# Merging normalizations into their consumers, moving one more copy of the heads to ScalarE, and batching small vector instructions

## What is computed

```python
x = x + 0.5 * moe(layernorm(x))         # 64 experts, top 8 of a sigmoid router, plus a shared expert
x = x + heads(layernorm(x))             # 16 heads of 8 features; softmax(y y^T / sqrt(8)) @ x, then a 2048 x 128 weight
x = x + 0.5 * moe(layernorm(x))
x = x + 0.5 * cells(layernorm(x))       # gated cell over 4 steps, then tanh output
x = x + decayed_attention(layernorm(x)) # with its own second normalization and a 128-512-128 mlp
x = x + 0.5 * cells(layernorm(x))
```

## Time and profile before

| what | value |
|---|---|
| median of three runs | 2742.0 us (2739.37 to 2742.69) |
| the profiled execution, time | 2743.51 us |
| its span | 2741.4 us |
| mean granted TensorE clock | 0.966 |
| PE, DVE, ACT, POOL busy | 93%, 81%, 66%, 45% of the span |
| moe normalization and routing, twice | from 5.85 to 88.3 us and from 1663.8 to 1740.2 us |
| experts, twice | to about 617 and 2269 us |
| heads, tiles | 657 to 1660 us |
| cells, twice; decayed attention; mlp | the rest |

### The profile page before, as it was taken

One profiled execution on the slowest core, in us unless ns is written; L12 is line 12 of the kernel. 1 busy time (PEld: TensorE's weight loads), 2 busy tenths in 40 slices (PEclk: granted clock), 3 DMA queues, 4 the chain that ended last, 5 costly groups with the idle time before them and its releaser, 6 DMA issues. The chain is left out here.

```text
span 2741.4 us, 35099 instructions
## 1 busy us (share of the span) xinstructions
PE 2545.0 (93%) x11075; PEld 1905.2 (69%) x11075; DVE 2223.1 (81%) x3277; ACT 1821.2 (66%) x3026; POOL 1231.3 (45%) x1265
## 2 busy tenths in 40 slices
PE   6899999996999999999999997899999998788778
PEld 3688888874666666666666664688888885476556
DVE  6778777776999999999999996777787775567655
ACT  3455555556888888888888884455555555557665
POOL 3466666664323232332323322466666662245401
PEclk9999999998999999999999999999999999888999
DMA  3566666644333333333333321566666640100000
GB/s 85 118 138 145 145 142 135 136 103 164 98 107 99 106 102 97 109 100 104 104 103 101 98 93 34 127 144 138 135 146 145 143 105 8 32 16 8 8 8 31
DMA packets 107385, 271.47 MB, mean 99 GB/s; under 512 B 30784, under 2 KB 35648, under 8 KB 107072
## 3 DMA queue, kind: packets, MB, share of 16 engines
q1 hardware_dynamic: 82192, 235.42, 34.7%
q0 software_dynamic: 24576, 33.62, 4.4%
q10 hardware_dynamic: 432, 0.20, 0.0%
HBM read 258.35 MB, written 10.76 MB: 98 GB/s over the span
## 5 line engine op out<-in xcount | busy, mean ns | idle before, releaser
L614 POOL TENSOR_TENSOR moe_experts_lo<-moe_experts_hidden,moe_experts_hi 128x512 fp32r<-128x512 f32 x512 | 661.1, 1291 | 340.6 <-ACT moe_experts_hi L552 340.4
L895 DVE TENSOR_TENSOR heads_e_lo<-heads_e,heads_e_hi 128x1024 fp32r<-128x1024 f32 x512 | 616.1, 1224 | 25.7
L559 ACT ACTIVATE psum<-psum 128x512 f32<-128x512 f32 x512 | 298.0, 582 | 479.8 <-PE psum L90 479.8
L729 POOL DMA_DIRECT2D heads_left<-heads_parts x512 | 306.5, 612 | 671.3 <-PE psum L783 610.7
L835 ACT ACTIVATE heads_e<-psum 128x1024 f32<-128x1024 f32 x512 | 520.0, 1023 | 108.2 <-PE psum L783 108.2
L586 DVE TENSOR_TENSOR moe_experts_weighted<-moe_spread,psum 128x512 f32<-128x512 f32 x512 | 350.8, 685 | 190.2 <-PE psum L90 186.4
L88 PE MATMUL psum<-heads_e_hi,heads_v_lo 128*128 128x512 f32 x1024 | 429.4, 419 | 18.0 <-DVE heads_u L861 18.0
L88 PE MATMUL psum<-moe_n_hi,moe_w_lo 128*128 128x512 f32 x1024 | 400.8, 391 | 4.2 <-PEq L54 3.9
L89 PE MATMUL psum<-heads_e_lo,heads_v_hi 128*128 128x512 f32 x1024 | 404.2, 395 | 0.0
L90 PE MATMUL psum<-heads_e_hi,heads_v_hi 128*128 128x512 f32 x1024 | 400.9, 391 | 0.0
L89 PE MATMUL psum<-moe_n_lo,moe_w_hi 128*128 128x512 f32 x1024 | 400.2, 391 | 0.0
(11 more groups left out here) (403 smaller groups left out, 4093.8 us busy)
## 6 DMA issues: line engine op xcount, KB each, us to landing
moe_spread<-moe_mask SPq DMA_DIRECT2D x128, 1024.0 KB, 9.8
heads_right<-heads_parts SPq DMA_DIRECT2D x512, 64.0 KB
heads_left<-heads_parts POOLq DMA_DIRECT2D x512, 64.0 KB, 2.5
heads_scale<-heads_inverse_copy SPq DMA_DIRECT2D x64, 512.0 KB, 3.7
moe_experts_raw<-in_gate SPq DMA_DIRECT2D x16, 256.0 KB, 11.7
moe_experts_raw<-in_up SPq DMA_DIRECT2D x16, 256.0 KB, 11.8
moe_experts_raw<-in_down SPq DMA_DIRECT2D x16, 256.0 KB, 11.6
heads_parts<-heads_e_hi SPq DMA_DIRECT2D x16, 256.0 KB, 3.2
```

The lines of the kernel that those rows point to most:

```text
L559: act.activation(psum[:, GATE + p % 2, :], psum[:, GATE + p % 2, :], ACT.Silu).then_inc(silu_ready, 1)
L614: pool.tensor_tensor(lo[:, p, :], hidden[:, p % 2, :], f(hi[:, p, :]), ALU.subtract).then_inc(low_ready, 1)
L729: eng.dma_start(f(tile[row:row + 2 * HEAD, h % 2, :]), parts_dram[dims, order:order + 2, at]).then_inc(loaded[h % 2], 16)
L895: dve.tensor_tensor(e_lo[:, s, :], e[:, s % 4, :], f(e_hi[:, s, :]), ALU.subtract).then_inc(low, 1)
```

## The change

- The normalization becomes a class `Norm` whose parts are called inside the stage that uses it, for routing, cells and mlp (five places). The heads and decayed attention keep the separate stage. Of its 8 PSUM banks it uses 6 (two for variances), and the stages' banks are arranged so that their first products find free ones. Chunk 0's low part moves from GpSimd to VectorE everywhere; in the moe layers the splits of the first experts' weights move behind the low parts.
- In routing, the first products run before the normalization's last chunks are done, the mask copy moves to ScalarE, and selection uses one instruction for four tiles where it used four (chosen, scaling); the sum of the best eight is a reduction of its own.
- In the heads, tile 4's high part moves from VectorE to ScalarE, and the three steps on u use one instruction of 1024 columns in place of two of 512.

```diff
 # normalization
-    BANKS = 4
-    VECTOR_LOWS = (2, 5, 7)
+    CENTERS, VARIANCES = 4, 2
+    VECTOR_LOWS = (0, 2, 5, 7)
+        for i in range(self.early):
+            split(i)
+        for c in range(CHUNKS):
+            if c not in self.VECTOR_LOWS:
+                self.take_low(pool, "pool", c)
+        for i in range(self.early, len(self.splits)):
+            split(i)
+    def wait_banks(self, eng):
+        eng.wait_ge(self.scaled_ready, CHUNKS)
+        eng.wait_ge(self.logs_taken, CHUNKS)
 # routing, TensorE
+                norm.tensor(pe)
+                norm.wait_weights(pe)
+                pe.wait_ge(norm.scaled_ready, LOGITS + 5)
                 logits(0, 0)
+                pe.wait_ge(norm.log_ready, CHUNKS)
+                shared(0, 0)
+                norm.wait_banks(pe)
                 turn_affinity(0, 0)
                 each_chunk(step)
 # routing, ScalarE
+                def copy_mask(c, j):
+                    act.wait_ge(routed_turned, c + 1)
+                    after(act, mask_stored[j], 16 * (c // 2))
+                    act.copy(mask[:, j, :], psum[0:EXPERTS, MASK, :]).then_inc(mask_ready, 1)
                 def step(c, j, last):
                     if not last:
                         affinities(c + 1, 1 - j)
+                    if c > 0:
+                        copy_mask(c - 1, 1 - j)
                     act.wait_ge(up_ready, c + 1)
 # routing, VectorE
-                    for q in range(4):
-                        dve.scalar_tensor_tensor(out=chosen[:, j, q, :], in0=rest[:, j, q, :], scalar=0.0,
-                                                 in1=scores(q), op0=ALU.is_lt, op1=ALU.mult,
-                                                 accum_out=total[:, j, q:q + 1]).then_inc(chosen_ready, 1)
+                    dve.tensor_reduce(total[:, j, :], best[:, j, :, :], mybir.AxisListType.X, ALU.add).then_inc(total_found, 1)
+                    dve.scalar_tensor_tensor(out=chosen[:, j, :, :], in0=rest[:, j, :, :], scalar=0.0,
+                                             in1=psum[:, TURNED + j, :].rearrange("p (q t) -> p q t", q=4)[:, :, 0:EXPERTS],
+                                             op0=ALU.is_lt, op1=ALU.mult).then_inc(chosen_ready, 1)
-                    for q in range(4):
-                        dve.tensor_scalar(routed[:, j, q, :], chosen[:, j, q, :], total[:, j, q:q + 1], None,
-                                          ALU.mult).then_inc(routed_ready, 1)
+                    dve.tensor_tensor(routed[:, j, :, :], chosen[:, j, :, :],
+                                      total[:, j, :].unsqueeze(2).to_broadcast([P, 4, EXPERTS]), ALU.mult).then_inc(routed_ready, 1)
-                    dve.tensor_copy(mask[:, j, :], psum[0:EXPERTS, MASK, :]).then_inc(mask_ready, 1)
 # heads
-        ACT_HIGH = (1, 3, 5, 7)
+        ACT_HIGH = (1, 3, 4, 5, 7)
-                    pe.wait_ge(u_low, (g + 1) * HALVES)
+                    pe.wait_ge(u_low, g + 1)
-                            after(pe, scaled_ready, (h - 1) * HALVES + half + 1)
+                            after(pe, scaled_ready, h)
-                    for half in range(HALVES):
-                        act.wait_ge(scaled_ready, g * HALVES + half + 1)
-                        act.copy(u_hi[:, g % 2, half, :], u[:, half, :]).then_inc(u_high, 1)
+                    act.wait_ge(scaled_ready, g + 1)
+                    act.copy(u_hi[:, g % 2, :], u[:, :]).then_inc(u_high, 1)
-                    for half in range(HALVES):
-                        after(dve, u_low, (g - 1) * HALVES + half + 1)
-                        dve.tensor_tensor(u[:, half, :], scale[:, g % 2, half * BANK:(half + 1) * BANK],
-                                          psum[:, OUT + half, :], ALU.mult).then_inc(scaled_ready, 1)
+                    after(dve, u_low, g)
+                    dve.tensor_tensor(u[:, :], scale[:, g % 2, :], psum[:, OUT:OUT + 2, :].rearrange("p a b -> p (a b)"),
+                                      ALU.mult).then_inc(scaled_ready, 1)
 # cells, TensorE
+        SUMS = ((6, 7, 4), (5, 0, 1))
+                norm.tensor(pe)
+                norm.wait_weights(pe)
+                norm.wait_banks(pe)
                 from_input(0)
 # mlp, TensorE
+                norm.tensor(pe)
+                norm.wait_weights(pe)
+                pe.wait_ge(norm.log_ready, CHUNKS)
                 up(0, 0)
+                norm.wait_banks(pe)
```

More of the change, by code:

```diff
@@ L128, in matrices @@
     return parts, [(dram[name], *parts[name]) for name in names]
-def layernorm(nc, tag, psum, consts, x, n_hi, n_lo, affine=None, keep=None,
-              splits=(), loads=(), copies=None, copied=None, x_dram=None):
-    center, inv, eps, columns = (consts[name] for name in ("center", "inv", "eps", "columns"))
+class Norm:
     CENTERED, VARIANCE = 0, 4
-    BANKS = 4
-    RING = 4
-    SCALES = 3
-    VECTOR_LOWS = (2, 5, 7)
-    with ExitStack() as ctx:
[L144 to L173, removed]
@@ new lines, in chunk, with wait_low, wait_weights @@
+    def chunk(self, c):
+        return slice(c * BANK, (c + 1) * BANK)
+    def wait_low(self, eng, c):
+        who = "vector" if c in self.VECTOR_LOWS else "pool"
+        eng.wait_ge(self.low_ready[who], sum((i in self.VECTOR_LOWS) == (c in self.VECTOR_LOWS) for i in range(c + 1)))
+    def wait_weights(self, eng, count=None):
+        eng.wait_ge(self.split_low, self.early if count is None else count)
+    def wait_banks(self, eng):
+        eng.wait_ge(self.scaled_ready, CHUNKS)
+        eng.wait_ge(self.logs_taken, CHUNKS)
@@ new lines, in tensor, with difference, variance @@
+    def tensor(self, pe):
+        def difference(c):
+            if self.x_loaded:
+                pe.wait_ge(self.x_loaded[c], 16)
+            after(pe, self.scaled_ready, c - self.CENTERS + 1)
+            pe.matmul(self.psum[:, self.CENTERED + c % self.CENTERS, :], self.consts["center"], self.x[:, self.chunk(c)],
+                      start=True, stop=True).then_inc(self.difference_ready, 1)
+        def variance(c):
+            pe.wait_ge(self.squares_ready, c + 1)
+            after(pe, self.logs_taken, c - self.VARIANCES + 1)
+            pe.matmul(self.psum[:, self.VARIANCE + c % self.VARIANCES, :], self.consts["inv"], self.squares[:, c % 3, :],
+                      start=True, stop=True).then_inc(self.variance_ready, 1)
+        for c in range(CHUNKS + 1):
+            if c < CHUNKS:
+                difference(c)
+            if c >= 1:
+                variance(c - 1)
@@ L177, in _ @@
             def _(sp):
[L178 to L188, removed]
@@ L263, in high @@
[L263 to L274 removed]
+                norm.vector(dve)
@@ L352, in down_product, with shared @@
                     product(pe, psum[:, DOWN + j, :], down, (hi[:, j, :], lo[:, j, :])).then_inc(down_ready, 1)
+                def shared(c, j):
+                    after(pe, added, c - 1)
+                    product(pe, psum[:, GATE + j, :], gate, (n_hi[:, tokens(c)], n_lo[:, tokens(c)]))
+                    product(pe, psum[:, UP + j, :], up, (n_hi[:, tokens(c)], n_lo[:, tokens(c)])).then_inc(up_ready, 1)
                 def step(c, j, last):
@@ L356, in step @@
                         logits(c + 1, 1 - j)
[L357 to L359 removed]
+                    if c > 0:
+                        shared(c, j)
                     if not last:
@@ L975, in _ @@
             def _(act):
-                act.wait_ge(cell_ready, HALVES)
-                for half in range(HALVES):
-                    act.copy(c_hi[:, half, :], cell[:, half, :]).then_inc(high_ready, 1)
+                norm.scalar(act)
                 for t in range(0, BATCH):
```

291 lines of the change are left out of this document (178 added, 113 removed).

## The result

The changed kernel takes 2811.22 us (median, 2809.79 to 2816.33) where the kernel before takes 2742.35 (2739.37 to 2743.34) beside it: a ratio of 1.0256 with a 95% interval of 1.0239 to 1.0274, or +69 us. The forecast was 2812 us, +70. Its profiled execution has a time of 2809.79 us and a span of 2808.0.

A forecast was written before the change was run, and what follows sets the result against it. It took the heads' TensorE to wait for u behind VectorE's queue, and routing to be bound by a four-engine chain and VectorE. +103 - 22 - 5 - 6 = +70 gave 2812 us; 8 in 10 range 2775 to 2836.

The forecast's parts named there:

- part 1: Heads: tile 0's rows wait for u 1.63 us longer in each of 63 heads, +103 us (+82 to +110).
- the 1.08 us for the cast: Heads: ScalarE's cast of tile 4 delays tile 5's cast and low part, so u starts 1.08 us later.
- the 0.54 for the single u: Heads: TensorE waits for u over 1024 columns, 1.22 us, not its first half, 0.68: 0.54 us per head.
- Rival A: Heads: VectorE is the bound, a lighter one serves u sooner, -32 us, total 2677; chance 0.11.
- D: Whole kernel: the two effects nearly cancel, ScalarE's second cast overlapping more than shown, 2742 to 2775; chance 0.04.
- B: Heads: TensorE's waits lower the granted clock, 2.4 us a head, +151, about 2963; chance 0.03.
- Routing: Routing and its normalization: earlier first selection, shorter start and chunks of 5.07 us, -11 us each (-7 to -13).
- the reserve of 0.7 us for GpSimd's late splits: Routing: 0.7 us taken off the gain for the last mask copy's DMA wait and late splits delaying the first shared low part.
- Cells: Cells: first product waits for the last scaling, not the stage's end: -2.4 us, twice -5 (-1 to -4 each).
- The mlp: Mlp: first product can start behind the last logarithm, at most -7.0; -6 us taken (-3 to -7).
- C: Heads as forecast, but merged stages give little, chunk length unchanged: 2833 us; chance 0.06.
- parts 2 and 3: Routing twice, -22 us together; cells -5 and mlp -6.

The follow-up runs named there:

- late_splits_last: merges_early with GpSimd's three late splits of the experts' weights moved behind the last three shared low parts of the routing: 2677.62 us, ratio 0.9775.
- heads_as_before: The changed kernel with both heads edits taken back (tile 4's cast on VectorE, u in halves): 2704.36 us, ratio 0.9863.
- merges_early: heads_as_before with the scaling of u one place forward in VectorE's queue, behind low part 4: 2681.38 us, ratio 0.9788.
- early_scaling: The changed kernel, five casts and single u kept, with the scaling of u moved behind low part 4: 2706.59 us, ratio 0.9874.
- select_by_four: heads_as_before with the routing's selection taken back to four instructions for chosen scores and four for scaling: 2715.28 us.
- cast_six: The changed kernel with ScalarE casting tile 6's high part in place of tile 4's: 2747.33 us, ratio 1.002.
- single_u_early: merges_early with the three steps on u in single instructions of 1024 columns: 2683.68 us, ratio 0.9792.
- before_five_casts: The kernel before with only tile 4's high part of the heads cast on ScalarE: 2808.86 us, ratio 1.0249.
- select_and_mask: heads_as_before with selection by four and the mask copy back on VectorE, normalization still merged: 2725.69 us.

## Why the prediction was right

The chain of part 1 is shown, by the timeline and by eight kernels that took links out of it or moved them. Point by point:

- The start of tile 0's rows at 7.37 us was measured as 7.36; the 1.08 us for the cast as 1.05 to 1.07, the 0.54 for the single u as 0.53 to 0.56 (differences of stages by 63), the head as 17.1. u over 1024 columns from PSUM lasted 1.22, its nearest row. VectorE fell to 85% and ScalarE to 85% (forecast 83 and 86).
- The range was held by following each engine's queue with durations of rows, not by shares. Rival A (a lighter VectorE serves u sooner) fell: in the trace VectorE gave up 24 us of 200 and stood for ScalarE. D fell with the sum of the two edits. B fell for these gaps: the granted clock in the heads is 1.00 with a gap of 1.47 us in each. The Trainium skill, "TensorE: Matmul & The Clock Gate", section "HAM oscillation — how this bites in real kernels", warns of waits between bursts; here, at this length, the trace doesn't show it.
- Routing was forecast at -11 per layer and came at -10.1 and -8.7. The chunk of 5.07 was right to the last digit, and the experts started at 78.03 (forecast 77). The term that was mis-sized is the reserve of 0.7 us for GpSimd's late splits: I had them delay the shared low part, but they held up VectorE's own scaling by 0.8 us. Then, from L505 of chunk 0 to that of chunk 1, it took 6.24 us (33.55 to 39.79), not 5.07, with VectorE standing 1.53 for the down product and TensorE partly at its low level (granted 0.77 from 32 to 36 us, 0.80 from 36 to 40). The low level doesn't need the hold-up: late_splits_last has none, its granted clock is 0.60 from 32 to 36 us all the same (1.00 from 36 on), and its step takes 5.61 us. The end, from the last L505 to the experts' table load, lasts 7.84 us where it took 6.93 before. What made up for part of this is that the first selection came at 30.24, 1.1 us earlier than the 31.3 of the prediction. The -8.7 is less firm than the -10.1: the second routing with its normalization, the same code, lasts 66.5 to 70.5 us in the eight kernels that have it (67.7 here).
- Cells: -3.1 and -0.7, not -2.5 each. In the second one the first product did come early, 18.99 us behind the table load (21.29 before), but TensorE's products ran at the low level until 2758.1, 5.9 us, where before they had done so for 3.5 (2687.15 to 2690.6). The 18 input products took 6.90 us in place of 5.82, so that the clock took 1.1 of the 2.3 us back; where behind them another 0.5 went, the stage alone doesn't show. The prediction named the clock's state there and bounded it with -1. The first one hides more than it shows: its first product came 3.5 us earlier from the table load (17.77, before 21.28), and its part behind the normalization lasts 54.2 us here and 52.1 in five kernels with the same code. The mlp: -6.9, not -6.
- Decayed attention was costed at zero and gave 5.7 us back. Its part behind the first normalization alone fell by 7.1, and no instruction of that part was changed; two kernels with the merged normalizations have it as long as before (last section). What decides is open. By size it is the largest error of the sum. The misses of routing and cells (+3.1 and +1.2) went the other way, so that the total came out closer than its terms deserve.
- C, that the merges give little, fell by heads_as_before, which is 36 us faster than the kernel before. That this is more than the 33 of parts 2 and 3 is luck too: the stages with merges gave 31 (10.5 and 10.0 in routing, 3.7 and 2.1 in cells, 4.9 in the mlp), and 4.3 came from decayed attention.

## What to carry to other kernels

Moving work to the less busy engine helps only if it isn't put ahead of something that the critical chain needs there: the same cast cost 68 us on tile 4 and nothing on tile 6. Before shifting or splitting work, ask of the instruction that the bound engine waits for whether it needs what stands ahead of it in its queue; here moving it one place forward was worth 105 us in the changed kernel, and 31 us in the heads even where its wait seemed to be 0.22 us. Price edits by stages that are cut at the same instruction in both traces, for untouched stages move too.

## What the hardware showed beyond what was expected

**A gap on TensorE costs more than its bracket says.** Tile 0's rows in heads_as_before, with the products ahead of them:

```profile
1013.16 0.51 PE L857 MATMUL psum<-heads_right,heads_left 32*128 32x512 f32 x4
...
1014.87 0.40 PE L90 MATMUL psum<-heads_u_hi,heads_w_hi 128*128 128x512 f32 x1
1015.49 0.47 PE L88 MATMUL psum<-heads_e_hi,heads_v_lo 128*128 128x512 f32 x1 [0.23 <-DVE heads_u L937]
1015.80 0.40 PE L89 MATMUL psum<-heads_e_lo,heads_v_hi 128*128 128x512 f32 x1
```

and in merges_early:

```profile
1001.16 0.51 PE L857 MATMUL psum<-heads_right,heads_left 32*128 32x512 f32 x4
...
1002.87 0.39 PE L90 MATMUL psum<-heads_u_hi,heads_w_hi 128*128 128x512 f32 x1
1003.10 0.40 PE L88 MATMUL psum<-heads_e_hi,heads_v_lo 128*128 128x512 f32 x1
1003.33 0.39 PE L89 MATMUL psum<-heads_e_lo,heads_v_hi 128*128 128x512 f32 x1
```

A matmul is shown 0.39 us long, but the next one starts 0.23 us behind it. The bracket counts from the end of the row, 0.16 us later than TensorE could have gone on. From row to row the wait is 0.62 - 0.23 = 0.39 us, and the first matmul behind it takes 0.31 to the next one in place of 0.23. Together 0.47 us per head, and the stage got 30.9 / 63 = 0.49 shorter (from one head's products to the next one's, 15.48 and 15.02 us). Gaps on TensorE are to be read from start to start. The excess is no constant, though: where early_scaling's `scores` wait for exponential 5 the bracket says 0.35, from start to start it is 0.42 (0.74 - 0.32), and its head of 15.38 us is 0.36 longer than that of merges_early. So a bracket may be short by nearly nothing or by half.

**VectorE and GpSimd exclude each other for whole instructions.** The rows are those of select_by_four and late_splits_last above: 1.14 us for four elements, 0.42 where no subtraction ran beside it and 1.21 where one did. An instruction with an operand in PSUM kept its length beside the next such subtraction: in heads_as_before L510 started at 34.30 and lasted 0.69 us as in every later chunk, GpSimd's subtraction running from 34.22 to 35.50. GpSimd waits in its turn: its subtraction at 29.85 of the changed kernel, which starts while VectorE's low part runs (29.33 to 30.31, two SBUF inputs), lasts 1.60 us in place of 1.26. The two meet in every later chunk too, where it costs nothing because VectorE then stands for the down product anyway: L486, four elements, lasts 0.33 us in place of 0.16 and ends at 43.21, 0.02 behind the end of GpSimd's low part (41.92, 1.27 long). The Trainium skill says in "SBUF — State Buffer", section "SBUF: two separate sides", that the port pair which the two engines share is locked for a whole instruction, and that of VectorE's instructions those with two SBUF inputs or in a two-port mode take part. The trace agrees: the long ones are a product of two SBUF tensors and scalings from SBUF to SBUF; whether the scalings ran in such a mode no row tells.

**A stage whose code is the same in all kernels lasts 202 to 210 us.** The part of decayed attention behind its first normalization, in cast_six and in single_u_early (columns as above, the eighth number is the granted clock):

```profile
2389.18:2591.24 202.06, 168.67 (x800) 137.82 (x800) 146.78 (x130) 127.18 (x192) 87.77 (x54) 0.88 0.03 11
```

```profile
2326.23:2535.66 209.43, 177.80 (x800) 146.53 (x800) 146.89 (x130) 127.46 (x192) 89.09 (x54) 0.83 0.03 11
```

The instructions are the same, 800 matmuls; TensorE is busy 9 us longer at a granted clock of 0.83, VectorE equally long. The profiles show 209.4 in the kernel before, 209.6 in before_five_casts, 202.3 in the changed kernel, 201.8 to 205.3 in nine others (cast_six among them) and 209.7 in select_and_mask. It isn't settled what in the earlier stages decides between them; each kernel was profiled once, and no run varied the start of the stage alone. What is shown is that such a stage can hide or feign 7 us, 0.3% of this kernel. The first cells behind their normalization do the same on a smaller scale: with equal code they last 52.1 us in five kernels, 54.2 in two (the changed one is one) and 55.0 in five.
